# A transformer layer with routed experts: turned columns, selections and places shared otherwise between ScalarE and VectorE

## The reference

```
x: 8 x 256 tokens, 256 features; ctx: 8 x 77 x 256; mask over the 77 context rows
q    = layernorm(x)
attn = softmax(where(mask, q @ ctx^T / 16, -9e15))
x    = x + layernorm(attn @ ctx) * gamma + beta
h    = layernorm(x)
p    = softmax(h @ w_gate)              # 8 experts; the best two are kept, renormalised
g, u = split(h @ w_gate_up[e])          # 256 -> 2 x 1024
out  = x + sum over the two experts of p[e] * ((silu(g) * u) @ w_down[e])
```

## Time and the profile before

| | |
|---|---|
| median of 3 runs | 473.14 us (472.71 to 473.88) |
| the profiled execution | 472.3 us, its span 470.3 us |
| busy: TensorE, VectorE, ScalarE, GpSimd | 431.9, 310.1, 225.0, 189.4 us |
| mean granted clock of TensorE | 0.971 |

### The profile page before, as it was taken

One profiled execution on the slowest core, in us unless ns is written; L12 is line 12 of the kernel. 1 busy time (PEld: TensorE's weight loads), 2 busy tenths in 40 slices (PEclk: granted clock), 3 DMA queues, 4 the chain that ended last, 5 costly groups with the idle time before them and its releaser, 6 DMA issues.

```text
span 470.3 us, 10470 instructions
## 1 busy us (share of the span) xinstructions
PE 431.9 (92%) x2318; PEld 352.6 (75%) x2319; DVE 310.1 (66%) x770; ACT 225.0 (48%) x488; POOL 189.4 (40%) x206
## 2 busy tenths in 40 slices
PE   4987676999999999999999999999999999999980
PEld 2866432778888888888888888888888888888870
DVE  0675897788587748776775548876875477755530
ACT  2485493465465436444544336545634365433330
POOL 4143522345345433553444433543444334533221
PEclk9799879999999999999999999999999999999997
DMA  7533471236435513552452212542452124211111
GB/s 199 201 97 108 123 240 57 62 112 167 123 86 140 129 26 71 153 123 62 129 152 31 42 23 71 154 126 71 118 154 34 34 67 112 33 36 23 13 22 11
DMA packets 29217, 43.91 MB, mean 93 GB/s; under 512 B 3399, under 2 KB 22832, under 8 KB 29200
## 3 DMA queue, kind: packets, MB, share of 16 engines
q1 hardware_dynamic: 19842, 31.94, 21.8%
q0 software_dynamic: 7520, 10.39, 13.1%
q10 hardware_dynamic: 1838, 1.39, 1.1%
HBM read 34.07 MB, written 9.64 MB: 93 GB/s over the span
## 4 chain that ended last, share of the span: by engine, by line
PE 81%; issue 5%; DVE 5%; POOL 3%; DMA 3%; ACTq 1%; SPq 1%; DVEq 0%; ACT 0%; POOLq 0%
PE bank L1294 46%; PE bank L1314 15%; PE bank L1316 8%; PE bank L1304 7%; DMA beta_c<-in_L_xattn_beta 2%; PE bank L1278 2%; POOL x_sb L478 1%; PE bank L1106 1%; PE bank L1151 1%; POOL att_scale L472 1%; DMA out<-y_sb,out_i 1%; DVE w L366 1%; ACTq L1029 1%; DVE token_sel L693 1%; PE bank L1137 1%
## 5 line engine op out<-in xcount | busy, mean ns | idle before, releaser
L1294 PE MATMUL bank<-w,tokT_hi 128*128 (+1 forms) x624 | 174.8, 402 | 4.2 <-DVE tokT_lo L817 3.2
L1046 ACT ACTIVATE gated<-bank,row_rstd 128x512 f32<-128x512 f32 x78 | 53.8, 689 | 184.1 <-PE bank L1294 183.7
L1294 PEld LDWEIGHTS bank<-w,tokT_hi 128*128 128x128 f32 x624 | 112.8, 189 | 28.6 <-issue 5.0
L1314 PE MATMUL bank<-w,aT_hi 128*128 (+1 forms) x312 | 119.5, 417 | 1.1 <-DVE y_sb L847 1.1
L826 DVE SCALAR_TENSOR_TENSOR act<-bank,row_rstd,gated 128x512 f32<-128x512 f32 x78 | 58.4, 749 | 85.0 <-ACT gated L1046 85.0
L546 POOL DMA_INDIRECT out<-y_sb,out_i x39 | 61.8, 1586 | 96.0 <-DVE y_sb L847 95.8
L1294 PE MATMUL bank<-w,tokT_lo 128*128 (+1 forms) x312 | 97.2, 393 | 0.0
L1316 PE MATMUL bank<-w,aT_lo 128*128 (+1 forms) x312 | 87.5, 280 | 0.0
L533 POOL TENSOR_TENSOR tok<-tok,beta_b 128x256 f32<-128x256 f32 x38 | 28.2, 743 | 110.0 <-DMA tok<-rows_d,gather_i 110.0
L1294 PEld LDWEIGHTS bank<-w,tokT_lo 128*128 128x128 f32 x312 | 58.8, 189 | 13.5
L1314 PEld LDWEIGHTS bank<-w,aT_hi 128*128 128x128 f32 x312 | 58.7, 188 | 12.1 <-issue 1.3
(11 more groups left out here) (160 smaller groups left out, 413.9 us busy)
## 6 DMA issues: line engine op xcount, KB each, us to landing
raw<-in_L_ffn_w_gate_up SPq DMA_DIRECT2D x32, 512.0 KB, 3.8
raw<-in_L_ffn_w_down SPq DMA_DIRECT2D x16, 512.0 KB, 3.9
rows_d<-x_sb SPq DMA_DIRECT2D x8, 264.0 KB, 2.1
x_sb<-in_x SPq DMA_DIRECT2D x8, 256.0 KB, 7.5
out<-x_sb SPq DMA_DIRECT2D x8, 256.0 KB, 2.6
out<-y_sb,out_i POOLq DMA_INDIRECT x39, 3.8
tok<-rows_d,gather_i POOLq DMA_INDIRECT x38, 4.1
vals<-in_ctx ACTq DMA_DIRECT2D x1, 462.0 KB
```

Source lines behind the costliest of these rows:

```text
L1046: act_e.activation(gated[:, h, :], ps_g[h][:, :], ACT.Silu, scale=row_rstd[:, s:s + 1]).then_inc(gated_set, 1)
L1294: ins = pe.matmul(ps[:, :], tokens_[:, s, k, :], w.rearrange("p a g d -> p (a g) d"), start=(k == 0 and tokens_ is tokT_hi and part == 0), ...
L1314: pe.matmul(ps_y[:, :], aT_hi[:, h, c, :], w.rearrange("p a t d -> p (a t d)"), start=(h == 0 and c == 0), stop=False, skip_group_check=True)
```

## The change

Gamma and beta are loaded as four rows of 128 features with two DMAs, and TensorE turns them into columns. TensorE's first instructions come in another order, with 4 spins at first for 12 and two pairs of spins between. In the attention loop VectorE makes the scaled values of batch i - 2 after the maximum of batch i + 1, ahead of the statistics, splits and choices; the negated maximum is made tile by tile, with the tile's scale as a scalar. GpSimd adds batch b to x before it makes the scale of batch b + 1. The groups are chosen a step earlier. Selections of tiles 0 to 13 are made one by one and multiplied with the token's number, so that places are plain ones and zeros: ScalarE makes them for tiles 0 to 13, with one Relu for a group, VectorE for tiles 14 and 15. The fourth to sixth weight pieces are loaded at batches 1 to 3 (before: 4 to 6).

`packed` is gone: VectorE works out for each block the column of the table that holds it, as a selection of 39 columns; ScalarE copies the table, TensorE turns it, ScalarE copies it again, and TensorE multiplies it with the selection. The two index lists follow at once, and the fourth low split comes after the first token tile.

```diff
-            for k in range(KD):
-                part = slice(k * P, (k + 1) * P)
-                sp.dma_start(gamma_c[:, k:k + 1], gamma[part].unsqueeze(1)).then_inc(cols_in, 16)
-                sp.dma_start(beta_c[:, k:k + 1], beta[part].unsqueeze(1)).then_inc(cols_in, 16)
+            sp.dma_start(cols_row[0:KD, :], gamma.rearrange("(k p) -> k p", p=P)).then_inc(cols_in, 16)
+            sp.dma_start(cols_row[KD:2 * KD, :], beta.rearrange("(k p) -> k p", p=P)).then_inc(cols_in, 16)
...
-                if 4 <= b < 4 + PIECES - RAW:
-                    load_piece(0, RAW + b - 4)
+                if 1 <= b < 1 + PIECES - RAW:
+                    load_piece(0, RAW + b - 1)
...
             for i in range(B // 2 - 1):
                 x_rstd(i)
-            scales(0)
-            x_rstd(B // 2 - 1)
-            for b in range(1, B):
+            for b in range(B):
                 scales(b)
-                x1(b - 1)
+                if b < B - 1:
+                    x1(b)
+                if b == 0:
+                    x_rstd(B // 2 - 1)
...
-                dve.scalar_tensor_tensor(out=neg_max[:, tiles(b)], in0=most[:, tiles(b)], scalar=-1.0, in1=rstd[:, tiles(b)],
-                                         op0=ALU.mult, op1=ALU.mult).then_inc(masked, 1)
+                for t in range(TPB * b, TPB * (b + 1)):
+                    dve.tensor_scalar(neg_max[:, t:t + 1], most[:, t:t + 1], rstd[:, t:t + 1], -1.0, ALU.mult, ALU.mult).then_inc(masked, 1)
...
-                dve.tensor_tensor(token_sel[:, 2 * g[0]:2 * (g[-1] + 1), :].rearrange("p (n c) q -> p n c q", c=2),
-                                  count_hi[:].unsqueeze(1).unsqueeze(1).to_broadcast([P, n, 2, P]),
-                                  hi[:, part, :].unsqueeze(3).to_broadcast([P, n, 2, P]), ALU.is_equal).then_inc(token_set, 1)
+                for t in g:
+                    if t < BY_ACT:
+                        for c in range(2):
+                            dve.tensor_scalar(token_sel[:, 2 * t + c, :], count_hi[:], hi[:, t, c:c + 1], number[:, t:t + 1],
+                                              ALU.is_equal, ALU.mult).then_inc(token_set, 1)
+                    else:
+                        dve.tensor_tensor(token_sel[:, 2 * t:2 * (t + 1), :], count_hi[:].unsqueeze(1).to_broadcast([P, 2, P]),
+                                          hi[:, t, :].unsqueeze(2).to_broadcast([P, 2, P]), ALU.is_equal).then_inc(token_set, 2)
...
+            def block_columns():
+                after(tables)
+                step(tables, dve.tensor_scalar(jump[:], padded[:], -1.0 / P, float(FULL), ALU.mult, ALU.add))
+                step(tables, dve.tensor_tensor(past[:], block_start[:].unsqueeze(2).to_broadcast([P, NBLK, E - 1]), per_block(ends, P), ALU.is_ge))
+                after(tables)
+                step(tables, dve.tensor_tensor(past_x[:], past[:], per_block(jump, P), ALU.mult))
+                after(tables)
+                step(tables, dve.tensor_reduce(column[:], past_x[:], X, ALU.add))
+                after(tables)
+                dve.scalar_tensor_tensor(out=column_sel[:], in0=column[:], scalar=part_no[:], in1=neg_block[:],
+                                         op0=ALU.subtract, op1=ALU.is_equal).then_inc(column_sel_set, 1)
...
-            ctx_means(1, 2, 4)
             bans(0, 0, 2)
             x_stats(0)
+            ctx_means(1, 2, 4)
...
-            for i in range(B + 2):
-                if i >= 3:
-                    scaled_values(i - 3, 0)
-                    scaled_values(i - 3, 1)
+            for i in range(B + 1):
                 if i + 1 < B:
                     masked_logits(i + 1)
+                if i >= 2:
+                    scaled_values(i - 2, 0)
+                    scaled_values(i - 2, 1)
                 if i < 3:
                     x_stats(i + 1)
-                if 3 <= i < 6:
+                if 3 <= i < 5:
                     split_low(dve, i - 3)
+                if i == 5:
+                    dve.wait_ge(const, 17)
+                    choose(GROUPS[0])
                 if i == 6:
-                    choose(GROUPS[0])
+                    slots(0, GROUPS[0])
+                    split_low(dve, 2)
                 if i == 7:
                     choose(GROUPS[1])
                 if i == 8:
-                    slots(0, GROUPS[0])
                     select(GROUPS[0])
...
-            places(2, range(BY_ACT, GROUPS[3][0]))
...
-                for t in g:
-                    part = place_sel(t)
-                    act_e.wait_ge(apart_set, 2 * (t + 1))
-                    act_e.activation(part, part, ACT.Relu, bias=number[:, t:t + 1], scale=neg_number[:, t:t + 1]).then_inc(place_set, 1)
+                part = (place_early if g[0] < NT // 2 else place_late)[:, 2 * g[0] % NT:2 * (g[-1] + 1 - g[0]) + 2 * g[0] % NT, :]
+                act_e.wait_ge(apart_set, 2 * (g[-1] + 1))
+                act_e.activation(part, part, ACT.Relu, bias=1.0, scale=-1.0).then_inc(place_set, 1)
...
-            act_e.activation(packed[:, 0:FULL], ps_token[:, 0:FULL], ACT.Copy).then_inc(packed_set, 1)
-            act_e.wait_ge(start_set, 1)
-            firsts = [act_e.value_load(start_i[0:1, e:e + 1], min_val=1, max_val=NBLK - 1) for e in range(1, E)]
...
+            act_e.activation(table[:], ps_token, ACT.Copy).then_inc(table_set, 1)
+            act_e.wait_ge(tableT_ps, 1)
+            act_e.activation(tableT[:], ps_tableT, ACT.Copy).then_inc(tableT_set, 1)
...
-                    spin(1, bank[7])
...
-            spin(12, bank[0])
+            spin(4, bank[0])
+            turn_x(0)
+            turn_ctx(0)
             pe.wait_ge(wg_in, 16)
...
-            turn_x(0)
-            turn_ctx(0)
+            pe.wait_ge(cols_in, 32)
+            pe.transpose(ps_cols, cols_row[:], ident[0:2 * KD, 0:2 * KD]).then_inc(cols_ps, 1)
+            spin(2, bank[3])
+            turn_x(1)
+            spin(2, bank[3])
+            logits(0)
             pe.wait_ge(wg_set, 2)
...
-            turn_x(1)
             gate_ctx(0)
-            logits(0)
...
+            pe.matmul(ps_tableT, table[:], ident_b[:], start=True, stop=True).then_inc(tableT_ps, 1)
+            spin(4, bank[2])
+            pe.wait_ge(tableT_set, 1)
+            pe.wait_ge(column_sel_set, 1)
+            pe.matmul(ps_packed, tableT[:], column_sel[:], start=True, stop=True).then_inc(packed_ps, 1)
```

More of the change, by code:

```diff
@@ L806, in _ @@
             after(tables)
[L807 to L809 removed]
+            block_columns()
             block_experts()
[L811 removed]
+            dve.wait_ge(packed_ps, 1)
+            step(index, dve.tensor_scalar(spare_at[:], ps_packed, 0.0, spare_no[:], ALU.is_equal, ALU.mult))
+            after(index)
+            dve.tensor_tensor(gather_i[:], ps_packed, spare_at[:], ALU.add).then_inc(gather_set, 1)
+            step(index, dve.tensor_tensor(row_f[:], ps_packed, spare_at[:], ALU.add))
+            after(index)
+            dve.tensor_scalar(out_i[:], row_f[:], -1.0, None, ALU.add).then_inc(out_set, 1)
             row_stats(0, 0, 0)
@@ L1077, in experts @@
                     split_due(act_e, pieces, split_high)
-            for e in range(1, E):
-                pack(e)
             tok_high(0, 0)
@@ L1242, in _ @@
                     ranks(1, GROUPS[1])
-            pe.wait_ge(token_set, 1)
-            spin(3, bank[2])
-            pe.wait_ge(token_set, 2)
-            spin(3, bank[2])
+            for n in range(0, 2 * GROUPS[2][0], 4):
+                pe.wait_ge(token_set, n + 1)
+                spin(2, bank[2])
             ranks(2, GROUPS[2])
```

102 lines of the change are left out of this document (47 added, 55 removed).

## The result

The changed kernel takes 466.53 us (median of 4 runs, 464.51 to 468.64), the kernel before 473.50 beside it (4 runs, 472.71 to 473.88): a ratio of 0.9855, 95% interval 0.9819 to 0.989. Forecast was 466.8. Two later sets of runs of the same changed kernel, on other chips, gave 466.22 (ratio 0.9871, 0.9835 to 0.9908) and 468.16 (0.9875, 0.9848 to 0.9902). The profiled execution shown here took 468.64 us with a span of 466.8; that of before took 472.3 with a span of 470.3. It is the slowest of its four runs, so it shows 3.7 of the 7.0 us (3.5 of span).

The account below looks back on a forecast made before the run. The expert loop (371 of 470.3 us, TensorE busy 357) was taken as the unchanged bound, only the first 99 us movable. Terms 2.9 + 0.5 + 2.9 = 6.3 gave 466.0, with 0.8 for the median 466.8 us; range 462.3 to 470.8.

Parts of the forecast that it names:

- Part 1: Front: columns by TensorE and an earlier x(1) bring the fourth row maximum 2.9 us forward, bounds 1.0 and 4.4.
- the low clock ends earlier in the work: Front: TensorE's stretch at low clock was to cover less of the work, supporting 2.9 us at the fourth row maximum.
- a fourth maximum later than 26: Front: a sign named beforehand, there written as maximum 3 later than 26 us, that would speak for rival (b).
- rival (b): Front and start give only their lower ends, x(1) at 11.3 and low clock at first products: 470.0 us, chance 0.20.
- Parts 2 and 3: Attention loop, selections and places: loop gains 4.0 us, mostly spent on work behind it; 0.5 us left, bounds -0.8 and +4.8.
- The walk: Attention loop: scaled values timed turn by turn from maximum 3 at 27.1 to scaled(6) at 53.0 us, 57.05 before.
- 45.2, 49.3, 53.0: Attention loop: forecast times in us of the last scaled values, up to scaled(6), with waits for collisions counted in.
- rival (a): Middle: the collisions between VectorE and GpSimd don't come, the middle gives 4.8 us, total 462.5 us; chance 0.20.
- Part 4: Expert loop's start: packed columns replaced, first product 1.6 us earlier, clock stays up; 2.9 us taken, ends 1.3 and 3.3.
- cover: Expert loop's start: index instructions end at 76.9 us, the first token tile lands at 76.8: cover 0, price 0.14 us.
- (c): Loop: the turn stays near 4.6 us and group 0's selection is pure addition, middle -3.4, total 470.7 us; chance 0.07.
- (d): Loop: GpSimd's serial circle collides once more each turn, 5.5 us a turn, middle -7.3, total 474.6 us; chance 0.05.

Follow-up runs that it names:

- e2_front: The kernel before with only the columns by TensorE and the front's new order: 472.36 us, ratio 0.998.
- e6_before_warm: The kernel before with 16 spins between the first batch's context turns and the wait for the expert weights' copies: 469.97 us, ratio 0.9893.
- e3_middle: The kernel before with only the new loop, GpSimd's order, selections and places: 470.03 us, ratio 0.9937.
- e1_again: The changed kernel run once more without any edit: 466.22 us, ratio 0.9871 to the kernel before.
- e9_after_again: The changed kernel run again unedited on another chip, as the measure for kernels beside it: 468.16 us, ratio 0.9875 to the kernel before.
- e5_warm: The changed kernel with eight spins in place of two ahead of the second batch's turns: 465.95 us, ratio 0.9826 to the kernel before.
- e8_gpsimd_order: The changed kernel with GpSimd's old order, scale of batch b ahead of the addition of batch b-1: 465.61 us, ratio 0.981 to the kernel before.

## Why the prediction was right, and where its steps were off

The number was right (466.8 against 466.53) and its mechanisms were there, but two of its three terms were mis-sized, one up and one down. That they made up for each other is luck. The three terms against the stages of the table:

**Part 1, the front: 2.9 forecast.** The arrivals were near: the multiplications at 7.90 (7.9 forecast), x(1) at 9.9 (9.4; its load was issued 1.8 us earlier, not 1.4), the first maximum at 14.6 (14.7). The step that failed is "the low clock ends earlier in the work". With the new front and no added spins the fourth maximum was at 27.41, 23.46, 27.59, 23.91, 25.58, 27.68 and 27.51, in the mean 26.2; with the old one at 27.16, 26.53 and 28.19, in the mean 27.3. That is 1.1 us, anything from -0.4 to +3.8 in a single execution; with so few executions the mean itself is known to about 1 us only. e2_front's runs say the same: 0.66 us, at most 2.2 by its interval. By the prediction's own sign (a fourth maximum later than 26) the execution shown first, at 27.41, spoke for rival (b). Rival (b)'s front, 1.0, was nearer, but its reason (x(1) at 11.3) was not the cause. That the rate is what makes the difference is shown by the same products taking 1.1 or 0.6 us, and by e6_before_warm, where spins alone moved this maximum by 3.45 us and the median by 4.3. What sets the rate in the new front is not shown: the pause ahead of x(1) and the eight spins fewer at the start both stand as reasons.

**Parts 2 and 3, the middle: 0.5 forecast, 2.4 measured** (45.9 in the three executions of kernels with both old parts and no spins; 43.1 to 43.7 in the five that have both new). The walk was right for the first turns (32.3 and 36.5 forecast, 32.65 and 36.60 measured: the split does win over the addition, which waits 0.92), and right on what the loop's gain is spent on. Behind the last scaled values it takes 19.1 us to the index, 16.0 before, and 19.5 was forecast. One selection takes 0.27 us (0.26 forecast), a collision 1.0 (1.3 taken). The step that failed is the later turns, "45.2, 49.3, 53.0": turns of 4.5, 4.1 and 3.7 us for the collisions in them. The collisions came, at 41.79, 45.71 and 49.38, but the turns took 3.84, 3.74 and 3.32: a wait of about 1 us fell mostly into time in which VectorE stood idle anyway (1.1 to 1.2 us in each of the three turns before). Of rival (a) that half is true. The Trainium skill (SBUF — State Buffer, "Who interferes with whom") says that whichever engine issues first holds the shared pair for the whole instruction and that a `tensor_scalar`, which has one tensor input, can take it in a two-port mode. This case agrees on both: 2.22 us for a 1.30 addition behind a split, 3.12 against 2.13 for eight one-input selections, and 0.72 in place of 0.17 for 39 elements (L912) beside GpSimd's addition of beta.

**Part 4, the start: 2.9 forecast, 1.4 at the first product, 2.2 at the second low tile, 1.5 at the third gate product (94.42) and 1.0 at the end in the profiled pair; 2.2 in the mean over all executions.** First product, cover and clock came as forecast, and the 24 products did gain their 1.5 us (5.7 in place of 7.3). The step that failed is that this gain was counted in full: from the first product on, VectorE's list ends nearly as late as before (statistics 12.02 us behind the index, 12.11 before), the moved split being part of it, and the third tile's statistics wait 0.63 us for GpSimd's addition of beta, which met a split. The gain at full rate shows in full only against executions such as e2_front's and e3_middle's.

**The sum.** 1.1 + 2.4 + 2.2 = 5.7 us by the table, 5.0 to 7.0 by the three medians; 6.3 was forecast. Rivals (c) and (d) are out: no turn of the new loop is over 4.6 us. What stays open: why the clock comes back after 3.4 us in one execution (e1_again) and after some 13.7 in another (the one shown first), with TensorE busy nearly all the time in both, and what the 12 first spins would do there; and whether the spread of the changed kernel's runs (464.5 to 469.4 us) is all from there. The profiled executions say so as far as they go (3.35 and 0.27 us of time for 3.95 and 0.27 of the fourth maximum), but no more than one execution in a set has a trace.

## What to carry to other kernels

Cut the trace at the events that end the stages, and take each stage from several executions before a term is believed: here one stage alone moved by 4 us between executions of the same kernel. A load that arrives earlier is worth little if TensorE then works at half rate behind the pause; look at the rate first. Filling the pause gave the kernel before 4.3 us; in the changed kernel the same gave nothing clear (465.95 against 466.22 and 466.53). Where GpSimd and VectorE share a loop, put GpSimd's long instruction where VectorE isn't in a two-input one, and not just behind the semaphore that releases both.

## What the runs showed of the hardware

The granted clock's row can miss the slow rate. In e9_after_again it reads 1.00 for 10 to 14 us, while two spins take 1.03 us (0.59 in e5_warm) and the window holds 17 products, against 19 in the changed kernel's first execution, where the row reads 0.50, and 34 in e5_warm. It is no single case: in every execution the row reads 1.00 from 4 to 5 us, while the four spins from 2.45 on in the new front take 1.89 us, and in e8_gpsimd_order it reads 1.00 for the two spins of 1.03 us at 8.09. The duration of a known product is the surer sign.

One and the same load of w_gate, second in its queue, let TensorE go on at 6.93, 7.22, 8.10, 9.17 or 9.50 us in executions of kernels that are equal up to there.

GpSimd's power of two columns, 0.70 us alone, lasted 1.53 in e8_gpsimd_order (at 43.67 us), where it starts 0.25 us behind a low split of 1.22: here even an instruction on two columns waits for the split's end.
